# Second normalisation on ScalarE, attention products ahead of its transposes, loop unrolled

## The reference

```python
mod = (_silu(c) @ wmod).reshape(16, 6, 1, -1)
sa, ca, ga, sb, cb, gb = ...                       # ga, gb: kept at least 0.25 in size
h = _layernorm(x) * (1 + ca) + sa                  # first normalisation
y = h + linear_attention(h, Wq, Wk, Wv, Wo, ...)   # elu(.)+1 on Q and K, 16 heads of 8
y = layer_norm(y, g1, beta1)                       # second normalisation: ny in the kernel
z = y + relu(y @ W1 + b1) @ W2 + b2
x = x + ga * layer_norm(z, g2, beta2)
h = _layernorm(x) * (1 + cb) + sb                  # fourth normalisation: n3 in the kernel
x = x + gb * time_mix(h, W_r, W_k, W_v, mu_r, mu_k)
```

## Time and profile before

| | us |
|---|---|
| device time, median of 3 runs | 176.39 (175.75 to 177.12) |
| the profiled execution | 175.55 |
| its span, first to last instruction | 173.8 |
| PE busy | 161.4 (93% of the span) |
| DVE busy | 138.5 (80%) |
| POOL busy | 106.9 (62%) |
| ACT busy | 106.8 (61%) |

### The profile page before, as it was taken

The page is one execution under the profiler, slowest core; times in us unless marked ns, Lnnn a source line. Parts: engine busy times, 40 slices in busy tenths (PEclk is TensorE's granted clock), DMA queues, the critical chain, the costliest instruction groups (busy, mean ns, idle before and its releaser), DMA issues.

```text
span 173.8 us, 4407 instructions
## 1 busy us (share of the span) xinstructions
PE 161.4 (93%) x1189; PEld 148.5 (85%) x1189; DVE 138.5 (80%) x616; ACT 106.8 (61%) x292; POOL 106.9 (62%) x234
## 2 busy tenths in 40 slices
PE   7998799999999999999999999999999999988371
PEld 7786789899999999999898989898999998968261
DVE  3747877989798979898989898998989788776642
ACT  3154483758494949493939495858677675572251
POOL 5234337585676767677777776876767657554621
PEclk9999999999999999999999999999999999999999
DMA  4619633001020201111111114020203020202101
GB/s 119 204 43 315 168 65 53 18 21 47 2 83 12 65 25 51 40 45 46 34 56 33 58 30 60 25 65 3 87 0 91 0 81 0 75 0 79 32 15 45
DMA packets 11937, 9.96 MB, mean 57 GB/s; under 512 B 1123, under 2 KB 10902, under 8 KB 11926
## 3 DMA queue, kind: packets, MB, share of 16 engines
q1 hardware_dynamic: 11456, 9.54, 20.1%
q10 hardware_dynamic: 438, 0.28, 0.6%
q0 software_dynamic: 32, 0.01, 0.0%
HBM read 7.69 MB, written 2.13 MB: 57 GB/s over the span
## 4 chain that ended last, share of the span: by engine, by line
PE 80%; DVE 8%; POOL 4%; issue 2%; DMA 2%; ACT 1%; SPq 0%; DVEq 0%; POOLq 0%; ACTq 0%
PE bank L745 14%; PE bank L778 14%; PE bank L734 8%; PE bank L816 4%; PE bank L857 4%; PE bank L764 4%; PE bank L739 4%; PE bank L826 4%; PE bank L863 4%; PE bank L900 4%; PE bank L831 3%; PE bank L685 3%; PE bank L768 3%; PE bank L887 2%; DMA gm_rows<-mod_rows_dram 2%
## 5 line engine op out<-in xcount | busy, mean ns | idle before, releaser
L745 PE MATMUL bank<-w,hid 128*128 128x128 f32 x256 | 33.3, 275 | 0.0
L778 PE MATMUL bank<-x1T,w 128*128 128x256 f32 x128 | 32.9, 380 | 0.0
L268 ACT ACTIVATE hT<-bank,modT 128x256 f32<-128x256 f32 x16 | 9.0, 565 | 36.2 <-PE bank L734 36.1
L745 PEld LDWEIGHTS bank<-w,hid 128*128 128x128 f32 x256 | 30.9, 192 | 0.0
L778 PEld LDWEIGHTS bank<-x1T,w 128*128 128x128 f32 x128 | 22.1, 190 | 3.5 <-DVE z L609 0.2
L353 POOL TENSOR_TENSOR rstd_n<-vare_n,power 128x2 f32<-128x2 f32 x32 | 22.6, 707 | 2.5
L351 POOL TENSOR_TENSOR vare_n<-mv_n,eps 128x2 f32<-128x2 f32 x32 | 6.4, 200 | 24.0 <-DVE mv_n L426 24.0
L432 DVE TENSOR_SCALAR ny<-bank,mv_ny,rstd_ny 128x128 f32<-128x128 f32 x32 | 11.7, 406 | 5.7 <-POOL rstd_ny L353 5.7
L281 ACT ACTIVATE keepT<-bank,modT 128x255 f32<-128x255 f32 x32 | 16.2, 561 | 0.0
L565 DVE SCALAR_TENSOR_TENSOR mixT<-bank,modT,keepT 128x256 f32<-128x256 f32 x32 | 13.8, 471 | 1.1 <-ACT keepT L281 1.1
L398 POOL TENSOR_TENSOR out_sb<-x,prod 128x256 f32<-128x256 f32 (+1 forms) x16 | 11.4, 711 | 4.8 <-DVE prod L538 2.5
(11 more groups left out here) (128 smaller groups left out, 462.9 us busy)
## 6 DMA issues: line engine op xcount, KB each, us to landing
gm_rows<-mod_rows_dram SPq DMA_DIRECT2D x16, 192.0 KB, 3.1
out<-out_sb SPq DMA_DIRECT2D x15, 128.0 KB, 1.9
bv_row<-bv_rows_dram SPq DMA_DIRECT2D x16, 64.0 KB, 3.0
w<-in_w SPq DMA_DIRECT2D x1, 512.0 KB, 5.1
x_all<-in_x SPq DMA_DIRECT2D x1, 384.0 KB, 4.8
kqvo<-in_kqvo SPq DMA_DIRECT2D x2, 128.0 KB, 2.7
wmod<-in_wmod SPq DMA_DIRECT2D x1, 256.0 KB, 4.9
mix_w<-in_mix_w ACTq DMA_DIRECT2D x1, 192.0 KB, 4.0
```

The lines of the kernel that those rows point to most:

```text
L745: last = nc.tensor.matmul(banks[6][:, c * D:(c + 1) * D], hid[:, f, c * 128:(c + 1) * 128], w2[:, f, :], start=False, stop=(f == FF - 1 an ...
L778: return nc.tensor.matmul(bank[:, f % 2 * L:(f % 2 + 1) * L], w1[:, f * 128:(f + 1) * 128], x1T[:, :], start=True, stop=True)
```

## The change

1. **ny moves from DVE to ACT.** ACT can only do `scale * y + bias` with columns, so it needs the bias `-mean * rstd`. DVE writes `minus_mean` (128x2) right behind mv_ny; POOL multiplies it by rstd_ny into `shift_ny` (128x2) right behind rstd_ny; ACT writes ny with two Identity instructions at the end of its step, behind tanh_r (in step 1: ahead of mod_rows).
2. **On PE the `u` products come ahead of the ny transposes**; the ny transposes now stand directly ahead of the K products, behind the n3 transposes and `u`.
3. **The loop is gone**: all 20 steps are written out on every engine, and run-time slices become constants.

The diff, cut to its core (the rest of it is the renaming of `(j, off)` to `t`):

```diff
+        minus_mean, shift_ny = sb("minus_mean", [128, NC]), sb("shift_ny", [128, NC])
...
-        def steps(eng, step):
-
-            for t in range(STEPS_DEEP + 1):
-                step(0, t)
-            with eng.Fori(STEPS_DEEP // 2, S // 2 - 1) as j:
-                for off in (1, 2):
-                    step(j, off)
-            for t in range(S - 1, S + STEPS_DEEP):
-                step(0, t)
...
+        def steps(step):
+
+            for t in range(S + STEPS_DEEP):
+                step(t)
...
@@ ACT, step, behind tanh_r
-                if isinstance(j, int) and t == 1:
+                if live(t - 1):
+                    need(act, shift_ok, sb_ + 1)
+                    need(act, x1T_mm, sb_)
+                    for c in range(NC):
+                        last = nc.scalar.activation(ny[:, c, :], banks[1][:, c * D:(c + 1) * D], ACT.Identity,
+                                                    scale=rstd["ny"][:, c:c + 1], bias=shift_ny[:, c:c + 1])
+                    last.then_inc(ny_ok, 1)
+                if t == 1:
                     act.wait_ge(gates_turned, 1)
                     nc.scalar.activation(mod_rows[:, :, :], banks[2][0:S, D:4 * D].rearrange("p (k d) -> p k d", k=3),
...
@@ POOL
+            def y_shift(s):
+                need(pool, minus_ok, s + 1)
+                need(pool, rstd_ok["ny"], s + 1)
+                need(pool, ny_ok, s)
+                nc.gpsimd.tensor_tensor(shift_ny[:, :], minus_mean[:, :], rstd["ny"][:, :], ALU.mult).then_inc(shift_ok, 1)
...
                 if y_first:
                     norm_scale("ny", sb_ + 1)
+                    y_shift(sb_)
...
-                if live(j, off - 1) and not y_first:
+                if live(t - 1) and not y_first:
                     norm_scale("ny", sb_ + 1)
+                    y_shift(sb_)
...
@@ DVE, step
+                def minus_y_mean():
+                    need(dve, mv_ok["ny"], sb_ + 1)
+                    need(dve, shift_ok, sb_)
+                    nc.vector.tensor_scalar(minus_mean[:, :], mv["ny"][:, :, 0], -1.0, None, ALU.mult).then_inc(minus_ok, 1)
...
                     norm_mv("ny", sb_ + 1)
+                    minus_y_mean()
...
-                if y_first:
-                    normalise("ny", ny, lambda c: y[:, c, :], sb_ + 1, ny_ok)
...
-                if live(j, off - 1) and not y_first:
-                    normalise("ny", ny, lambda c: y[:, c, :], sb_ + 1, ny_ok)
...
@@ PE, step
-                if live(j, off - 2):
-                    need(pe, ny_ok, sd + 1)
-                    need(pe, hida_ok, sd)
-                    transpose_in(banks[7], ny, x1T_mm)
...
                         last = nc.tensor.matmul(banks[1][:, c * (D + H):(c + 1) * (D + H)], qT[:, c * 128:(c + 1) * 128],
                                                 kvs[:, :], start=True, stop=True)
                     last.then_inc(u_mm, 1)
-                if live(j, off):
+                if live(t - 2):
+                    need(pe, ny_ok, sd + 1)
+                    need(pe, hida_ok, sd)
+                    transpose_in(banks[7], ny, x1T_mm)
+                if live(t):
```

More of the change, by code:

```diff
@@ L236, in _, with step @@
             sp.wait_ge(rows_stored, 16)
-            def step(j, off):
-                if not isinstance(j, int) or off > 0:
-                    load_bv(j, off + 1)
-                load_gm(j, off - 2)
-                store(j, off - 4)
-            steps(sp, step)
+            def step(t):
+                if t > 0:
+                    load_bv(t + 1)
+                load_gm(t - 2)
+                store(t - 4)
+            steps(step)
             sp.wait_ge(stored, 16 * (S + 1))
@@ L273, in step @@
                                          bias=beta1_b2[:, :]).then_inc(x1T_ok, 1)
-                if live(j, off - 4):
+                if live(t - 4):
                     need(act, mix_ok, sc)
                     need(act, h2T_mm, sc + 1)
-                    if isinstance(j, int) and sc == 0:
+                    if sc == 0:
                         act.wait_ge(shift_cols, 2)
-                    nc.scalar.activation(keepT[:, :, 0:1], modT[:, FIRST:FIRST + 2, bass.ds(sc, 1)], ACT.Copy)
+                    nc.scalar.activation(keepT[:, :, 0:1], modT[:, FIRST:FIRST + 2, sc:sc + 1], ACT.Copy)
                     for i in range(2):
@@ L326, in step @@
                                          ACT.Copy).then_inc(rows_ok, 1)
-            steps(act, step)
+            steps(step)
             act.wait_ge(last_ok, 2)
@@ L545, in step_end, with step @@
                                                        ALU.mult).then_inc(prod_ok, 1)
-                if live(j, off - 2) and not z_first:
+                if live(t - 2) and not z_first:
                     norm_mv("z", sd + 1)
-            def step(j, off):
-                t = 2 * j + off
+            def step(t):
                 sa, sb_, sd, sp_, sc = t, t - 1, t - 2, t - 3, t - 4
@@ L659, in step @@
[L659 to L661 removed]
+                if live(t - 3) and not (t == S + 1):
+                    take_n3(t)
+                if live(t):
                     need(dve, a_ok, sa + 1)
[L663 removed]
+                    need(dve, bv_in[t % 2], 16 * (sa // 2 + 1), 16 * S)
                     need(dve, kv_mm, sa + 1)
[L665 removed]
+                    nc.vector.scalar_tensor_tensor(kv_raw[:, :], bv_row[t % 2][:, :], ksum, banks[3][:, 0:D],
@@ L673, in step @@
                     shift_columns()
-            steps(dve, step)
-            step_end(0, S + STEPS_DEEP - 1)
+            steps(step)
+            step_end(S + STEPS_DEEP - 1)
         @block.tensor
@@ L845, in step @@
                     hidden_product(2)
-                if live(j, off - 1):
+                if live(t - 1):
                     need(pe, att_ok, sb_ + 1)
@@ L902, in step @@
                     last.then_inc(v_mm, 1)
-                if live(j, off - 2) and not z_first:
-                    if draining(j, off):
+                if live(t - 2) and not z_first:
+                    if draining(t):
                         need(pe, hidb_ok, sd + 1)
                     feed_forward_out(2, FF).then_inc(z_mm, 1)
-            steps(pe, step)
+            steps(step)
 def kernel(**inputs):
```

299 lines of the change are left out of this document (145 added, 154 removed).

## The result

The changed kernel takes longer: a median of 183.34 us (182.35 to 184.98, 4 executions) against 176.27 (175.75 to 177.12) for the kernel before, a ratio of 1.0405 (95% interval 1.0319 to 1.0492). Measured again, on another chip, it took 182.33 (181.69 to 183.40, 6 executions) against 177.29 (175.78 to 177.87) for the kernel before, ratio 1.0309 (1.0261 to 1.0358). The forecast was 180.8, in a range of 177.2 to 184.3. So the direction and the range hold; the loss is +7.1 in the first measurement and +5.0 in the second, where +4.4 was worked out. Ratios leave out executions that the chip disturbed, so a ratio can differ a little from the quotient of two medians.

The account below looks back on a forecast made before the run. PE was taken as the bound, busy for all of the steady 9.01 us step. Terms 0.62 + 0.15 + 0.36 + 2.1 + 1.18 summed to 4.4 us, giving 180.8 on the median 176.39; range 177.2 to 184.3.

Parts of the forecast that it names:

- No gain from a lighter DVE: Steady step: taking ny's 0.73 us from DVE only lengthens its idle time before stats_z; gain 0.
- ny on ACT takes 0.81: ACT: two 128-column Identity instructions out of PSUM take 0.81 us for the pair, bounds 0.64 and 1.02.
- shift_ny 0.20 plus a hop: POOL: the new 128x2 piece takes 0.20 us and, with 0.08 to the next start, costs 0.28, hidden in the steady step.
- The moved transposes make attT late by 0.19 a step: Steady step: later ny transposes delay x1T and ACT's queue up to attT; PE stalls 0.19 us a step, bounds 0 and 0.37.
- The rival in which ACT's queue absorbs it: ACT closes up by 0.2 us between x1T and attT; only the edges cost 2.3, total 178.7; chance 0.17.
- ny late for `u`: Rival: ny's pair costs 1.02 us, hops 0.1 each; PE stalls 0.1 to 0.2 a step; 6.7 in all, 183.1; chance 0.10.
- PE waiting at u for ny: Sign that the forecast is wrong: PE stands at the `u` products for ny, where a slack of some 0.2 us was claimed.
- the term of steps 5 to 15, 11 x 0.19 = 2.1: Steps 5 to 15: a PE stall of 0.19 us before L739, waiting for attT, paid in each of 11 steps, 2.1.
- Steps 2 to 4, 1.13: First steps: later ny, hT, `u` and attT cost 0.62 us in step 2, 0.15 in step 3, 0.36 in step 4.
- Step 16, 1.18: Step 16 and after: x1T and L778 0.90 us later behind `u`, plus 0.28 for shift_ny ahead of rstd_n on POOL.
- Step 17 and after, 0: Step 17: ny transposes come behind n3's, but its z is wanted later than the rstd_n chain; price 0, bounds 0 and 1.
- late ny with step 17's bound: Upper end of the range: 7.9 us slower, from ny reaching `u` late (6.7) with step 17's upper bound (1).

## Why the prediction was right, and where it was not

- *No gain from a lighter DVE.* Right. DVE's idle time before stats_z, over all steps, is in the waits of the kernel after (us in total, times, longest); before it was 6.0 in 13 times.

```profile
DVE stats_z L425 <- PE bank L754: 16.5, 15, 1.3
...
PEld bank L748 <- ACT attT L294: 2.6, 12, 0.4
...
PE bank L820 <- ACT ny L321: 1.6, 3, 1.2
```

- *ny on ACT takes 0.81.* Right to the digit (0.81 a pair, 453 ns mean of one). The estimate of 0.4 from the page "Perfetto Trace Analysis" of the Trainium skill, section "Optimizing Scalar/DVE Operations", would have been half of it. *shift_ny 0.20 plus a hop:* right; minus_mean takes 0.17.
- *The moved transposes make attT late by 0.19 a step.* Right: the order alone gives 9.20, and so does the changed kernel once wv_gate is short. The rival in which ACT's queue absorbs it is out (L748 waits 12 times).
- *ny late for `u`.* The prediction gave `u` a slack of some 0.2 and this rival a chance of 0.10. It came true in part, by a mechanism that the rival did not name: the pair costs 0.81, not 1.02, but ny's end comes at +0.30 instead of +0.12, behind the longer pair `x`, and the load of `u` follows it by 0.11 where 0.05 was taken. It costs 0.07 to 0.15 a step. The listing alone would have hidden it: it has this wait three times, in steps 2 to 4. "PE waiting at u for ny" was one of the prediction's own signs of being wrong.
- *The step that failed is the term of steps 5 to 15, 11 x 0.19 = 2.1.* It measured 4.1. Its sentences were that `u` has slack for ny and that "k_sb and mixT come some 0.17 later, within their slack". I moved DVE's work in time and kept its durations. But 0.2 to 0.3 later it meets POOL's wv_gate, and the pair of `x` pieces grows from 0.61 to 0.81 or 1.09; ny, and in the longer case mixT too, is then late by more than its slack. The short wv_gate gives 1.9 of the 2.0 back (103.29 to 101.44). That the total fell inside the range although this term was half of what it measured owes something to the width of the range, and to the 0.5 that came back at the end.
- *Steps 2 to 4, 1.13.* Right in size (+1.1), in step 2 by another road than I named. The K products of step 2 start 7.92 after `u` of step 1 with mod_rows ahead of ny (13.42 to 21.34), and 7.90 with ny first (14.58 to 22.48, in the run with the old order in the drain); before, it is 7.42 (14.06 to 21.48, the latter in the earlier trace rows). So hT behind mod_rows is not what holds them alone; ny is enough, for which `u` stands 1.16 us. Step by step the loss is 0.5, 0.3 and 0.3 for the 0.62, 0.15 and 0.36 of the sum. The store of mod_rows was rightly priced at nothing.
- *Step 16, 1.18.* Measured 1.3. About half of it (0.6) is the order on PE.
- *Step 17 and after, 0.* Measured -0.5. The kernel before loses 1.20 there to the row load [the row at 159.90 above]; the load starts 2.7 us before the work ahead of xb is through (156.00, 158.69). In the second profile of the kernel after it starts 3.3 us before that (162.39, 165.71), since step 17 itself is slower there, and xb doesn't wait at all. With the old order in the drain it is 2.7 again, and the wait is back at 1.24. A cost in one place was partly paid by a wait that was there already.
- *Unrolling, 0.* Right: 9.00 instead of 9.01, and a gain of 0.2 to 0.8 us in all.
- *The total.* 4.4 forecast, 5.9 at full clock between the two profiles. In the first measurement, with +7.1, the mean clocks are 0.981 to 0.991, where five of the six executions of the second have 1.000; the one of them that was traced lost 2.6 to the clock.
- *The range.* Its upper end takes 7.9 for "late ny with step 17's bound"; 6.7 + 1 is 7.7, so the range is 0.2 wider than its own terms.

Why do the steps change from 9.28 to 9.56 at step 10? In that step DVE starts mv_ny 0.55 us after qT, where it takes 0.32 in the others (102.85 and 103.40; 93.57 and 93.89). The pause of 0.23 makes ny late, `u` of step 11 stands for it and starts at +0.67, and from there on the pair `x` meets wv_gate at its first moment. The second kind then keeps itself up: ny releases `u`, behind which come the ny transposes, x1T, exp_k, k_sb, the longer pair and the next ny. With wv_gate short, the same pause makes one step of 9.32, and the next takes 9.21 again; with ny alone moved it makes the one of 9.25. So here the pause starts the long steps, and the overlap keeps them; with attT ahead of hid 0 they start at step 6, without a pause. The same pause stands in step 10 of every version with ny on ACT that was traced, and in none with ny on DVE. What pauses there stays open.

## What to carry to other kernels

When work moves by a few tenths of a microsecond, look not only at who waits for it but at what it will now run beside: here a DVE instruction with two SBUF inputs and a POOL instruction stretched each other, so its duration is not a constant of the sum. After one late result has been found, ask for the second behind it, since removing the first can show a loss as large. A list of waits leaves the short ones out: a result that is followed by its reader at the same distance in every step, the distance at which it follows where the wait is plain, is waited for. And an engine's queue of DMA starts is an order like any other: a load that stands behind a store waits for whatever the store waits for, and an extra buffer alone does not help it.

## What the runs showed of the hardware

**Contention of DVE and POOL.** One 128x128 piece of `x` on DVE, with two full SBUF inputs, takes 0.345 us (the median of the steady steps before, and with the short wv_gate) or 0.54 (that of the kernel after; at most 0.63). A pair takes 0.61 us with half a POOL piece beside it, 0.60 with a wv_gate of 8 columns and k_pair's start, 0.81 where the full wv_gate starts 0.1 to 0.2 behind it, and 1.09 with POOL busy from its first moment; by the sum that is one piece stretched, and both. POOL's wv_gate goes the other way: 0.62 when DVE's pair is already running, 0.46 when they start together.

**From a result on ACT to PE.** The weight load of `u` starts 0.10 to 0.12 us behind the end of ny in every step in which it waits for it, and its matmul 0.03 behind the load, where it is 0.10 to 0.11 without a wait.

**The clock.** After a pause of PE the granted clock can fall from 2.4 to 1.2 GHz for some microseconds, and one execution of a kernel shows it where another doesn't. In the first profile of the kernel after, PE idles 1.36 us before `u` of step 1 (0.64 in the second profile, 0.59 before; 1.23 in the run with three buffers, which has no fall there), runs on at full clock for some 1.1 us, and is then at half until some 19 us; it is at half again after 1.16 us of idle time in step 2, where the second profile has 1.17 and stays at full clock:

```profile
14.57 0.73 PE L820 MATMUL bank<-kvs,qT 128*128 128x144 f32 x4 [1.36 <-issue]
...
22.66 1.30 PE L820 MATMUL bank<-kvs,qT 128*128 128x144 f32 x4 [1.16 <-ACT ny L321]
```

```profile
15.70:17.00 1.30, 1.30 (x6) 0.68 (x5) 1.27 (x8) 0.67 (x2) 0.90 (x3) 0.51 1.05 302
...
23.00:25.00 2.00, 2.00 (x10) 1.93 (x10) 0.91 (x7) 0.88 (x2) 0.43 (x2) 0.50 0.05 12
```

That stretch takes 35.62 us instead of 33.07, a price of 2.6. In step 17 of the run with the short wv_gate two pauses stand close together, and the eight pieces behind them take 3.17 where the second profile of the kernel after has 1.99 after the same pauses:

```profile
158.22 0.44 PE L744 MATMUL bank<-ident,n 128*128 128x128 f32 x2 [1.12 <-DVE n L441]
...
159.53 3.17 PE L787 MATMUL bank<-x1T,w 128*128 128x256 f32 x8 [0.66 <-ACT x1T L266]
```

The same two pauses, within 0.01, lead to a fall in the profiles of three versions (attT ahead, the short wv_gate, both) and to none in both profiles of the kernel after and in that with mod_rows ahead. Likewise L773 behind a pause of 2.79 takes 1.19 with the old order in the drain, and the same product behind 2.77 takes 0.67 in the kernel before. So each of these falls stands behind a pause, and the length of the pause does not decide it. Of the version that loads its rows early, all six executions ran at a mean clock of 0.995 to 1.000; whether that is because its PE waits less isn't shown, since the four with the order alone changed, and more waiting, ran at 0.999 to 1.000.
